# Delta attention on one core: four subtractions and a clamp on DVE become one masked addition, and ACT takes the gate as the bias of four exponentials

## The reference

```python
g_cum = jnp.cumsum(gc, axis=-1)
g_diff = g_cum[..., :, None] - g_cum[..., None, :]
decay = jnp.exp(jnp.tril(g_diff))
L = -jnp.matmul(kbc, jnp.swapaxes(kc, -1, -2)) * decay      # strictly lower part
attn = solve_triangular(eye - L, eye, lower=True)
v_intra = attn @ vbc
k_cumdecay = attn @ (kbc * jnp.exp(g_cum)[..., None])
# then for every chunk, with a state carried on:
a_i = (q_i @ k_i.T) * decay_i
v_new = v_i - k_cumdecay_i @ state
out_i = (q_i * exp(g_i)) @ state + a_i @ v_new
state = state * exp(g_last) + (k_i * exp(g_last - g_i)).T @ v_new
```

## Time and profile before

| | us |
|---|---|
| median of 3 runs | 2108.01 |
| lowest and highest | 2105.53, 2108.33 |
| the profiled execution | 2104.88 |
| its span, first to last instruction | 2103.1 |
| PE busy in the span | 1863.1 |
| DVE busy | 1287.3 |
| POOL busy | 1072.8 |
| ACT busy | 998.3 |

### The profile page before, as it was taken

How to read it: one execution, slowest core, us unless ns; L and a number is a source line. 1 busy time by engine, 2 the same in 40 slices (tenths; PEclk the granted TensorE clock), 3 DMA queues, 4 the chain that set the end, 5 groups by cost and what they waited for, 6 DMA issues and landing times.

```text
span 2103.1 us, 45860 instructions
## 1 busy us (share of the span) xinstructions
PE 1863.1 (89%) x16855; PEld 1192.4 (57%) x16855; DVE 1287.3 (61%) x2490; ACT 998.3 (47%) x2433; POOL 1072.8 (51%) x2252
## 2 busy tenths in 40 slices
PE   8779898786869876799999999999999999999987
PEld 5412465432224534444777777777777777677766
DVE  2634455486629641453777777777777777777753
ACT  3356132124511233342666566656665666566643
POOL 0530122221120031131878888878888888888863
PEclk8899899798889898799999999999999999999989
DMA  5033422200020323110222222222222222222221
GB/s 152 1 101 103 150 46 40 69 1 1 1 104 1 85 71 109 53 39 18 60 61 53 53 63 60 59 54 56 62 57 55 56 61 64 52 54 62 49 43 32
DMA packets 229261, 121.36 MB, mean 58 GB/s; under 512 B 141712, under 2 KB 208817, under 8 KB 228785
## 3 DMA queue, kind: packets, MB, share of 16 engines
q1 hardware_dynamic: 223424, 109.06, 20.5%
q0 software_dynamic: 5616, 9.38, 2.2%
HBM read 84.88 MB, written 36.68 MB: 58 GB/s over the span
## 4 chain that ended last, share of the span: by engine, by line
PE 25%; POOL 18%; issue 5%; SPq 3%; DVE 2%; ACT 2%; DMA 2%; POOLq 0%; DVEq 0%; ACTq 0%
POOL a_z L2574 7%; POOL a_term L2570 7%; PE ps L2022 6%; PE ps L2221 3%; PE ps L2032 3%; SPq L1955 2%; PE ps L2252 1%; POOL a_rstd L2546 1%; POOL a_xnorm L2552 1%; DMA a_l<-a_v_dram 1%; PE ps L2188 1%; SPq L1963 1%; PE ps L2197 1%; PE ps L2066 1%; PE ps L2139 1%
## 5 line engine op out<-in xcount | busy, mean ns | idle before, releaser
L2574 POOL TENSOR_TENSOR a_z<-a_z,a_term 32x14 f32<-32x14 f32 (+6 forms) x896 | 352.9, 394 | 70.2
L2570 POOL TENSOR_TENSOR a_term<-a_z,a_l 32x14 f32<-32x14 f32 (+6 forms) x896 | 333.2, 372 | 70.3
L2600 DVE SCALAR_TENSOR_TENSOR a_qkv<-a_raw,a_taps,a_qkv 128x1024 f32<-128x1024 f32 x192 | 247.2, 1288 | 6.1
L2022 PE MATMUL ps<-all_xn,a_w_qkv 128*128 128x512 f32 x512 | 247.2, 608 | 0.0
L842 POOL DMA_INDIRECT f_sums<-a_y,a_xs x23 | 36.0, 1567 | 197.7 <-ACT a_y L792 194.7
L2221 PE MATMUL ps<-a_out_t,a_w_out 128*128 128x256 f32 x512 | 130.6, 399 | 2.0 <-ACT a_out_t L2444 1.7
L2022 PEld LDWEIGHTS ps<-all_xn,a_w_qkv 128*128 128x128 f32 x512 | 89.2, 193 | 69.4 <-issue 67.6
L2365 ACT ACTIVATE a_raw<-ps 128x512 f32<-128x512 f32 x128 | 76.4, 599 | 108.7 <-PE ps L2022 108.0
L2032 PE MATMUL ps<-a_w_z,all_xn 128*128 128x256 f32 x512 | 122.6, 383 | 0.0
L2564 POOL COPY a_z<-a_l 32x256 f32<-32x256 f32 x64 | 27.0, 422 | 157.2 <-DMA a_l<-a_v_dram 156.7
L388 POOL DMA_INDIRECT f_rows<-a_row,a_slots x32 | 36.4, 1137 | 137.3 <-DVE a_of_tile L377 128.0
(11 more groups left out here) (331 smaller groups left out, 4277.3 us busy)
## 6 DMA issues: line engine op xcount, KB each, us to landing
a_gc_rows<-a_g_dram SPq DMA_DIRECT2D x64, 256.0 KB, 4.8
a_v_dram<-a_v SPq DMA_DIRECT2D x64, 256.0 KB
a_w<-in_f_w SPq DMA_DIRECT2D x24, 512.0 KB, 7.7
a_w_qkv<-in_a_w SPq DMA_DIRECT2D x16, 512.0 KB, 3.8
a_t_dram<-a_z SPq DMA_DIRECT2D x512, 8.0 KB
a_xs<-f_rows SPq DMA_DIRECT2D x46, 130.0 KB, 2.2
a_w_z<-in_a_w SPq DMA_DIRECT2D x16, 256.0 KB, 2.8
a_w_out<-in_a_wo SPq DMA_DIRECT2D x16, 256.0 KB, 3.1
```

Source lines behind the costliest of these rows:

```text
L2022: mm = pe.matmul(ps[:, to, :], w_qkv[:, k, mt * P:(mt + 1) * P], xn[:, k, b * T:(b + 1) * T], start=k == 0, stop=k == KC - 1)
L2570: pool.tensor_tensor(term[:, 0:j, j + 1:], z[:, 0:j, j:j + 1].broadcast_to([HP, j, n]), rows[:, j:j + 1, j + 1:].broadcast_to([HP, j, n]), ...
L2574: pool.tensor_tensor(z[:, 0:j, j + 1:], z[:, 0:j, j + 1:], term[:, 0:j, j + 1:], ALU.add).then_inc(sub_step, 1)
L2600: dve.scalar_tensor_tensor(to, rows, tap, to, ALU.mult, ALU.add).then_inc(conv_ready if j == TAPS - 1 else conv_step, 1)
```

## The change

DVE no longer subtracts the source's gate. One instruction adds `floor` to the four rows of `gc_rows`: `low` is g_cum of the target where the pair counts, and about -1e30 elsewhere. ACT makes the exponential in four instructions, one for each row, with the negated gate as the bias per partition. For this the gates of kind K_GC are negated once, before the loop and after the last other use of them. `low_ready` now counts 1 for a chunk instead of 4, and `decay_ready` is raised by the last of the four exponentials.

```diff
@@ load_gates (SP)
-                        sp.wait_ge(low_ready, PR * (w - 1))
+                        sp.wait_ge(low_ready, w - 1)
@@ make_decay (ACT)
-                    act.wait_ge(low_ready, PR * (w + 1))
-                    act.activation(decay[:, :, :], low[:, :, :], ACT.Exp).then_inc(decay_ready, 1)
+                    act.wait_ge(low_ready, w + 1)
+                    for r in range(PR):
+                        last = act.activation(decay[:, r, :], low[:, r, :], ACT.Exp, bias=gate(K_GC, w, r))
+                    last.then_inc(decay_ready, 1)
@@ make_low (DVE)
-                    for r in range(PR):
-                        dve.scalar_tensor_tensor(low[:, r, :], gc_rows[:, w % 2, r, :], gate(K_GC, w, r), floor[:, :],
-                                                 ALU.subtract, ALU.min).then_inc(low_ready, 1)
+                    dve.tensor_tensor(low[:, :, :], gc_rows[:, w % 2, :, :],
+                                      floor[:, :].unsqueeze(1).broadcast_to([P, PR, P]), ALU.add).then_inc(low_ready, 1)
@@ before the loop (DVE)
                 dve.wait_ge(g_step, 7)
+                dve.tensor_scalar(kind(K_GC), kind(K_GC), -1.0, None, ALU.mult)
                 dve.tensor_scalar(kind(K_NEG), kind(K_NEG), -1.0, None, ALU.mult).then_inc(gates_ready, 1)
```

## The result

The changed kernel takes 2130.99 us (median of 6 runs, 2128.38 to 2138.39), the kernel before 2106.77 us in runs of its own (6, 2101.95 to 2110.55). The ratio is 1.0142, with a 95% interval from 1.0118 to 1.0165: slower, by more than the 0.2% that a measurement can tell. The ratio is the one recorded for all runs together and not the quotient of the two medians, which is 1.0115; in the experiments the two differ by up to 0.0013. The forecast had the direction and not the size: +24 us by the medians, +30 by the ratio, instead of +12.8, and 2131 lies outside the range that ended at 2129. The profiled execution took 2129.19 us with a span of 2127.1, which is 24.0 us more than the profiled one of before.

A forecast was written before the change was run, and what follows sets the result against it. A loop of PE and POOL, once per head, was taken as the bound. Heads 12.2 us, plus 1.0 at the end, minus 0.45 in the lead-in, gave +12.8 us: 2119 us, range 2104 to 2129.

The forecast's parts named there:

- the two mechanisms: ACT's four exponentials end later, +0.55 us per turn, and DVE's new `low` slows POOL, 0.2 us per turn.
- the full loss in 8 of 14 heads: Heads where POOL has no pause from turn 2 to the next turn 1: 1.15 us each, 9.2 together.
- The loop of PE and POOL as the bound: Delta attention: PE and POOL wait for each other once per head; POOL is entered through `decay` or `low`.
- The term for the port: POOL beside the new two-source `low` on DVE: 0.2 us lost per `low`, between 0 and 0.35, three per head.
- The term for the exponentials: `decay` on ACT: four exponentials take 1.18 us instead of one of 0.633, +0.55 per turn, bounds +0.45 and +0.65.
- Where ACT's delay enters: Turn 2 takes the whole +0.55 us through v0, turn 0 +0.4; in turns 3 and 1 DVE's gain nearly cancels it.
- The slack of the other heads: Six heads lose less: four by turn 0 0.6 us each, one by turn 3 0.4, one staying on PE 0.2.
- The way into PE: A later POOL reaches PE in turn 1 through xnorm; that wait grows from 9.0 us to some 20.
- The ends: Last turns, bound by POOL, lose 1.0 us; the lead-in gains 0.45 us from DVE's shorter first `low`.
- The shift in time: Rival: POOL starts later and meets fewer of DVE's conv instructions, -0.85 us per head, 2097 us; chance 0.11.
- the length of DVE's list: Rival: DVE's turns set the pace, so 62 x 0.7 = 43 us go, to 2065; chance 0.03.
- the new `low` was not free: Denies the no-change rival: `low` costs POOL nothing and half of ACT's delay vanishes, 3.4 us, 2111; chance 0.19.

The follow-up runs named there:

- experiment 1: Kernel before with the changed kernel's single long mask on DVE and one exponential without bias, the gate left out: 2101.60 against 2089.12 us, ratio 1.0066.
- experiment 10: Kernel before with one more 32x56 product per substitution on POOL, written to a spare tile: 2111.39 against 2104.42 us, ratio 1.0040.
- experiment 6: Kernel before with four exponentials (bias zero) in turns 3, 0 and 1, and one in turn 2: 2114.03 against 2105.11 us, ratio 1.0042.
- experiment 2: Kernel before, its four subtractions kept, with the exponential in four with a zero bias in every turn: 2107.26 against 2089.12 us, ratio 1.0081.
- experiment 3: Changed kernel with its mask in four additions of 128x128 instead of one of 128x512: 2102.08 us against 2089.12 of the kernel before, ratio 1.0075.

## Why the prediction was wrong in its size, step by step

The direction and the two mechanisms were right, the sum was not. Two of its steps failed. The forecast took 0.2 us per `low` for POOL, and 0.36 to 0.40 was measured; and it counted the full loss in 8 of 14 heads only, and all 13 that I can measure got longer, by 1.45 us on average. By its own terms (8 x 0.6 + 4 x 0.2 + 0.4 and the ends) the mask would cost 6.0 us and ACT 6.6; experiment 1 has 13.9 for the mask, and from there to the changed kernel it is 0.75% more, some 16 us for ACT.

- **The loop of PE and POOL as the bound: right.** A dose of POOL work alone makes the kernel slower (experiment 10), and less work on DVE in one long instruction does too (experiment 1). That DVE's 0.7 us per turn would win nothing was right as well.
- **The term for the port: right in kind, too small.** The step put 0.2 us per turn between bounds of 0 and 0.35, "since not every POOL instruction meets it from its start". Measured is 0.36 (0.40 in experiment 1), just above the upper bound. POOL works through most turns and its instructions are short, so that one begins inside nearly every `low` and waits for its end: POOL loses over 0.2 us beside each of the 50 `low` from 1060 to 1960 us. I should have taken the row of qg in the earlier trace rows at its word: the small addition had lost 0.4 us there. With 0.38 in place of 0.2, eight heads give 3 x 0.18 x 8 = 4.3 us more.
- **The term for the exponentials: too small.** 0.55 was taken from k_row, 0.65 was measured, the upper bound; 0.8 us more in eight heads. The error lay in carrying over a row of another kind: k_row reads PSUM and has a scale, `decay` reads SBUF and has a bias. Which of the two it is, no run tells apart.
- **Where ACT's delay enters: right for the changed kernel, in too few heads.** The forecast had it in turn 2 for eight heads. The chain after passes turn 2's four exponentials in all 15. With the old `low` there is a second way, t_wide in turn 1 (2.4 us of waits before, 10.7 with four exponentials), and experiment 6 costs 0.42% by it and by 1.8 us of PE's clock. In the changed kernel this way is closed by the earlier `low` (2.5 us), and the forecast was right that the two nearly cancel there. By the chain, then, ACT's half enters mostly by turn 2: 15 x 0.65 = 9.8 us, an estimate, and 1.8 for the clock, of some 16. The chain is one execution's; a run of the changed kernel with one exponential in turn 2 alone, which would test it, was not made.
- **The slack of the other heads: wrong.** I gave six of 14 heads 0.2 to 0.6 us, because POOL paused in them for its DMA. On average that made 0.9 us per head; 1.45 was measured. I counted in them only the delay of the turn before which POOL paused. But the pause that I showed was 0.24 us, and my own terms for what comes ahead of it in the head are 0.55 + 0.2: the pause is used up, and the head loses what the others lose. That is argued; what the rows show is that the chain goes by turn 2 in 15 heads instead of 6, that the waits for the DMA are in 19 places instead of 25, and that all 13 heads take 70.8 to 71.6 us (before, 69.3 to 70.6). The measured terms of the full way, 0.65 + 3 x 0.36, give 1.73 us per head, an estimate; 1.45 was measured, so some slack was left.
- **The way into PE: half of it missed.** The forecast had PE's wait for xnorm go from 9.0 us to some 20. It is 12.8 in the same stretch. The larger part came at L2077: DVE waits for xnorm before xf (99.7 us against 55.2), behind xf stand its convolutions and the addition to x, and PE waits for that. A later xnorm is late twice. (With four exponentials alone, in experiment 2, PE's wait for xnorm falls to 1.4 us and the one at L2077 still grows to 16.5.) The row of that wait, 8.0 us, stood in the list before, but the earlier trace rows left it out.
- **The ends: +1.0 and -0.45 expected.** From the first `low` (899.85 us after, 901.00 before) to the first row of my measure it takes 3.2 us more, clear of the 0.2 us by which two profiles of the kernel before differ there. 1.8 of it are the matmuls at the lower clock, for which the forecast had no term. The last stretch is 3.1 us longer, but two profiles of the kernel before differ by 5.5 in it: nothing can be read from that.
- **The rivals.** The shift in time did not take POOL out of DVE's way, the length of DVE's list did not count, and the new `low` was not free.

Still open: what part of the mask's cost comes from DVE's later work moving rather than from POOL's time, and why shorter convolutions, which give POOL 0.8 us per turn, win nothing. The runs show that the next wait takes over, and not a rule for which one.

## What to carry to other kernels

Before merging several short DVE instructions into one long one, look at what POOL does beside it: if POOL works in small instructions and is on the path, the merged one can save 0.7 us on DVE and still cost more than it saves. Sum the busy time of an engine whose instructions did not change, before and after; here two rows of POOL showed one of the two causes at once. Count in how many rounds of a loop the chain takes each way, in the kernel before and in the changed one: here 6 of 15 became 15 of 15. And a pause of the engine that bounds is slack only up to its length: held against the delays ahead of it, 0.24 us is nothing.

## What the runs showed of the hardware that was not expected

- With its products and additions beside it, POOL lost per turn 0.45 us to one tensor_tensor of 128x512, 0.25 to four of 128x128, and 0.09 to four scalar_tensor_tensor of 128x128. These are my own sums over the rows of POOL's timeline: for every POOL instruction that ends within the DVE group or 0.25 us behind it, its length less the usual one of its shape. The differences agree with those of the substitution times (0.36, 0.12 to 0.19, 0), of which only the first is beyond the scatter. Why the slower form hurts least, I have not tested.
- DVE pays too: its four small instructions took 1.14 us with POOL quiet and 1.38 beside it.
- PE's granted clock fell from 1.00 to 0.51 between 990 and 995 us in the changed kernel, and four matmuls of 128x512 took 3.78 us instead of 1.98. The waits of PE ahead of it were 1.6, 0.4 and 0.4 us, against 1.4, 0.4 and 0.5 before. In experiment 3 they were 1.8, 0.4 and 0.5 and the clock stayed at 1.00, so the waits alone do not say when it falls.
- The same work in shorter instructions is cheaper for POOL: three convolutions of 128x1024 per turn, cut in halves, cost DVE 27 us more (274.1 against 247.2 for the group) and give POOL 52.6 us back.
- Exponentials of 128x128 from SBUF with a bias per partition take 0.40 us each and 1.28 for four; k_row's copies from PSUM with a scale per partition 0.38 and 1.14.
